# Score banks that accumulate on with differences of keys in four of eight rounds of a chunk

## What is computed

```python
h = _ln(x, g1, be1)
x = _attn(h, h, Wq1, Wk1, Wv1, Wo1, bo1) + x          # self-attention, 1024 keys
h = _ln(x, g2, be2)
x = _attn(h, context, Wq2, Wk2, Wv2, Wo2, bo2) + x    # cross-attention, 64 keys
h = _ln(x, g3, be3)
a, gate = split(h @ Wp + bp)
x = a * gelu(gate) @ W2 + b2 + x
```

## Time and profile before

| | |
|---|---|
| median of 3 runs | 2003.01 us (2002.07 to 2003.58) |
| the profiled execution's own time | 2002.8 us |
| its span, first to last instruction | 2001.0 us |
| PE / DVE / ACT / POOL busy, share of the span | 99% / 69% / 56% / 74% |
| granted TensorE clock | 1.000 |

### The profile page before, as it was taken

How to read it: one execution, slowest core, us unless ns; L and a number is a source line. 1 busy time by engine, 2 the same in 40 slices (tenths; PEclk the granted TensorE clock), 3 DMA queues, 4 the chain that set the end, 5 groups by cost and what they waited for, 6 DMA issues and landing times.

```text
span 2001.0 us, 32764 instructions
## 1 busy us (share of the span) xinstructions
PE 1990.7 (99%) x12568; PEld 1397.1 (70%) x12568; DVE 1382.0 (69%) x2766; ACT 1127.5 (56%) x1914; POOL 1489.8 (74%) x800
## 2 busy tenths in 40 slices
PE   9999999999999999999999999999999999999999
PEld 7665666666665666765666666665669999888888
DVE  6687687676767785587687666757767888744443
ACT  6565566554556665465566554556656776533332
POOL 3699899978989998899899889989897675300000
PEclk9999999999999999999999999999999999999999
DMA  8201000001000000010000001000030520000100
GB/s 275 85 32 38 6 7 17 8 25 48 17 12 6 17 6 27 1 64 6 7 18 10 27 1 53 7 27 1 22 104 10 158 69 1 1 22 28 37 12 32
DMA packets 48956, 67.19 MB, mean 34 GB/s; under 512 B 6176, under 2 KB 42144, under 8 KB 46752
## 3 DMA queue, kind: packets, MB, share of 16 engines
q1 hardware_dynamic: 48800, 65.10, 10.2%
HBM read 45.17 MB, written 19.92 MB: 33 GB/s over the span
## 4 chain that ended last, share of the span: by engine, by line
PE 94%; POOL 3%; DVE 2%; issue 1%; ACT 1%; DMA 0%; SPq 0%; POOLq 0%; DVEq 0%
PE score L559 21%; PE score L542 17%; PE score L685 9%; PE score L546 6%; PE score L497 5%; PE attn_project L699 5%; PE attn_project L670 5%; PE score L640 4%; PE attn_project L497 4%; PE first_score L523 4%; PE score L509 3%; PE attn_project L523 2%; POOL acc L1489 2%; PE score L608 2%; PE attn_project L608 2%; PE attn_project L509 2%
## 5 line engine op out<-in xcount | busy, mean ns | idle before, releaser
L1489 POOL TENSOR_TENSOR acc<-acc,pT 128x1024 f32<-128x1024 f32 x384 | 917.6, 2389 | 54.7 <-POOL acc L1489 1.3
L1233 ACT ACTIVATE pT<-score 128x1024 f32<-128x1024 f32 x512 | 525.3, 1027 | 141.1 <-PE score L546 100.3
L542 PE MATMUL score<-qk 64*128 64x512 f32 x3072 | 460.1, 399 | 0.4 <-ACT pT L1233 0.4
L559 PE MATMUL score<-pT,vT 128*64 128x512 f32 x1952 | 432.3, 595 | 0.0
L873 DVE TENSOR_REDUCE nmax<-first_score 128x1 f32<-128x512 f32 x512 | 347.8, 679 | 1.9 <-PE first_score L523 1.5
L873 DVE TENSOR_REDUCE nmax<-attn_project 128x1 f32<-128x512 f32 x512 | 347.7, 679 | 0.0
L542 PEld LDWEIGHTS score<-qk 64*128 64x128 f32 x3072 | 263.0, 185 | 107.5 <-ACT pT L1233 59.1
L559 PEld LDWEIGHTS score<-pT,vT 128*64 128x64 f32 x1952 | 134.6, 137 | 265.5 <-issue 245.4
L867 DVE SCALAR_TENSOR_TENSOR qk<-score,qk 128x512 fp32r<-128x512 f32 x66 | 45.6, 690 | 302.2 <-ACT qk L1214 302.2
L523 PE MATMUL attn_project<-qk 64*128 64x512 f32 x512 | 205.2, 401 | 3.4 <-DVE qk L867 3.4
L546 PE MATMUL score<-shift,pick 64*128 64x512 f32 x1024 | 208.4, 389 | 0.0
(11 more groups left out here) (196 smaller groups left out, 3135.8 us busy)
## 6 DMA issues: line engine op xcount, KB each, us to landing
xres<-x_middle SPq DMA_DIRECT2D x10, 512.0 KB, 3.7
raw_qk<-in_L_xattn_Wq SPq DMA_DIRECT2D x32, 128.0 KB, 2.3
raw_qk<-in_L_xattn_Wk SPq DMA_DIRECT2D x32, 128.0 KB, 2.5
raw_v<-in_L_xattn_Wv SPq DMA_DIRECT2D x8, 512.0 KB, 4.7
keys_all<-keys SPq DMA_DIRECT2D x1, 4096.0 KB, 13.1
values_all<-values SPq DMA_DIRECT2D x1, 4096.0 KB, 14.1
out_x<-xres SPq DMA_DIRECT2D x7, 512.0 KB, 2.9
xres<-in_x SPq DMA_DIRECT2D x3, 1024.0 KB, 6.6
```

The lines of the kernel that those rows point to most:

```text
L542: e.matmul(bank, qk[P % 2][r, 2 + h, keys], qk[P % 2][r, w, queries], start=(part == 0), stop=False)
L559: last = e.matmul(banks[bank][head * DH:(head + 1) * DH, :], vT[:, v_slot(D, jt), c0:c0 + DH], pT[:, jt, head, :], start=(jt == 0), stop=( ...
L1233: e.activation(pT[:, jt].rearrange("p h n -> p (h n)"), SC[R % 2][:, :], ACT.Exp).then_inc(s.exponential, 1)
L1489: e.tensor_tensor(total, total, pT[:, jt], ALU.add).then_inc(s.probs_added, 1)
```

## The change

A softmax numerator is `exp(score - max)`. In rounds 0, 1, 4 and 5 of a chunk the bank is started afresh and gets the shift, as before. In rounds 2, 3, 6 and 7 the same bank, which after the exponential still holds the shifted scores of the key tile two before, is not cleared: three pairs of matmuls with the **difference** of the key tiles (keys of jt minus keys of jt - 2) are accumulated on top, and the shift is not added again.

For this the split of a half of keys is made in more steps. ACT copies the first 256 columns in full to a new tile `keys_full`, and all 512 as leading parts (used by the rough scores and by the fresh tiles). DVE takes the rest of the first 256 columns, and subtracts `keys_full` from the last 256 columns in the PSUM bank. ACT rounds these differences, and DVE takes their rest. The queries' split stays as it was. The keys' projection moves from S1b to T1 and the sums' product from T1 to S1b, and to the head of the slot. Tiles are laid out anew, and three small ones are shared or cut (`ones`, `stats`, the order of `shift`).

```diff
@@ def slot(C):
+            if 1 <= C < NC - 1:
+                jobs += [("sum", C - 1, "S1b")]
             jobs += [(*job, through[i % len(through)]) for i, job in enumerate(between)]
             after = P + 1 + c
             if after < B * PAIRS:
-                jobs += [("qk", after, 1 - c, "S1b")]
-            if 1 <= C < NC - 1:
-                jobs += [("sum", C - 1, "T1")]
+                jobs += [("qk", after, 1 - c, "T1")]
             if after < B * PAIRS:
                 jobs += [("qk", after, 3 - c, "PJ")]
@@ first_score, tensor
-                need.wait_ge(s.split_hi, qk_of[P, half])
+                need.wait_ge(s.keys_rounded, keys_of[P, half])
@@ score, tensor
+                fresh = jt % TPC < 2
...
-                    e.matmul(bank, qk[P % 2][r, 2 + h, keys], qk[P % 2][r, w, queries], start=(part == 0), stop=False)
-                else:
+                    last = e.matmul(bank, key_part(P, h, r, jt), queries1[P % 2][r, w, c * BANK:(c + 1) * BANK],
+                                    start=(fresh and part == 0), stop=(not fresh and part == len(TERMS) - 1),
+                                    skip_group_check=not fresh)
+                elif fresh:
...
-                    e.matmul(bank, pick[r, :], shift[r, :], start=False, stop=True).then_inc(s.scored, 1)
+                    last = e.matmul(bank, pick[r, :], shift[r, :], start=False, stop=True)
+                if part == len(TERMS) - (0 if fresh else 1):
+                    last.then_inc(s.scored, 1)
@@ vector
+            def change_keys(P, u, bank):
+                n, later = keys_of[P, u], banks[bank][:, PAIR:]
+                need.wait_ge(s.keys_rounded, n)
+                need.wait_ge(s.keys_copied, n)
+                e.tensor_tensor(keys_lo[P % 2][:, u, 0:PAIR], banks[bank][:, 0:PAIR],
+                                keys_hi[P % 2][:, u, PAIR:2 * PAIR].bitcast(F32), ALU.subtract)
+                e.tensor_tensor(later, later, keys_full[:, :], ALU.subtract).then_inc(s.keys_changed, 1)
+                need.wait_ge(s.keys_changed, n)
+                need.wait_ge(s.split_hi, qk_of[P, u])
+                e.tensor_tensor(keys_lo[P % 2][:, u, PAIR:], later, keys_hi[P % 2][:, u, 0:PAIR].bitcast(F32),
+                                ALU.subtract).then_inc(s.split_lo, 1)
@@ split_qk, scalar, for keys
+                need.wait_ge(s.keys_changed, keys_of[P, u] - 1)
+                e.copy(keys_full[:, :], banks[bank][:, 0:PAIR]).then_inc(s.keys_copied, 1)
+                e.copy(keys_hi[P % 2][:, u, PAIR:], banks[bank]).then_inc(s.keys_rounded, 1)
+                need.wait_ge(s.keys_changed, keys_of[P, u])
+                e.copy(keys_hi[P % 2][:, u, 0:PAIR], banks[bank][:, PAIR:]).then_inc(s.split_hi, 1)
```

More of the change, by code:

```diff
@@ L118, in block_kernel @@
         maxima = sb("maxima", [PART, 2, SQUARE])
-        ones = sb("ones", [PART, DH])
+        keys_full = sb("keys_full", [PART, BANK // 2])
         QB = BANK // SQUARE
@@ L123, in block_kernel @@
         rsum = sb("rsum", [PART, QB])
-        (oT, pT, vT, acc, _, qk1, sums, qk0, shift, maxima_T, raw_qk, wqk, raw_v, wv, wo1) = overlay(
+        (oT, pT, vT, acc, shift, qk1, sums, qk0, maxima_T, raw_qk, wqk, raw_v, wv, wo1) = overlay(
             ("oT", [PRING, N], F32),
@@ L141, in block_kernel, with key_part @@
             ("wo1", [PAIRS, DIM], F32R))
-        qk = (qk0, qk1)
+        PAIR = BANK // 2
+        queries1 = [tile[:, 0:2 * N].rearrange("p (w n) -> p w n", w=2) for tile in (qk0, qk1)]
+        keys_lo = [tile[:, 2 * N:3 * N].rearrange("p (c n) -> p c n", c=CHUNKS) for tile in (qk0, qk1)]
+        keys_hi = [tile[:, 3 * N:].rearrange("p (c n) -> p c n", c=CHUNKS) for tile in (qk0, qk1)]
+        def key_part(P, w, r, jt):
+            c, t = divmod(jt, TPC)
+            start = t * PART if w else (t + 2) % TPC * PART
+            return (keys_lo if w else keys_hi)[P % 2][r, c, start:start + PART]
         _, *places = overlay(("oT_kept", [PRING, N], F32),
@@ L276, in block_kernel @@
         qk_of = numbered((P, u) for P in range(B * PAIRS) for u in (0, 2, 1, 3))
+        keys_of = numbered((P, u) for P in range(B * PAIRS) for u in range(CHUNKS))
         def rows_there(key):
@@ L411, in rouse @@
                 for _ in range(n):
-                    e.matmul(banks["S1b"][0:DH, 0:DH], ones[:, :], ones[:, :], start=True, stop=True)
+                    e.matmul(banks["S1b"][0:DH, 0:DH], sums[:, 0, 0:DH], sums[:, 0, 0:DH], start=True, stop=True)
             def context_turn():
@@ L522, in first_score @@
                 for m, (w, h) in enumerate(FIRST):
-                    last = e.matmul(banks[bank], qk[P % 2][r, w, q0:q0 + PART],
-                                    qk[P % 2][r, 2 + h, half * BANK:(half + 1) * BANK],
+                    last = e.matmul(banks[bank], queries1[P % 2][r, w, q0:q0 + PART], keys_hi[P % 2][r, half, PAIR:],
                                     start=(m == 0), stop=(m == len(FIRST) - 1))
@@ L732, in _ @@
                         sum_quads(C - 1, "T0")
-                    for part in range(len(TERMS) + 1):
+                    for part in range(len(TERMS) + (jt % TPC < 2)):
                         for head in range(2):
@@ L776, in ln_stats @@
             def ln_stats(src, mv_of, key):
-                n, slot = stat_of[key], key[1] % TILES
-                need.wait_ge(s.ln_agg, n - TILES if n > TILES else 0)
+                n, slot = stat_of[key], stat_of[key] % TPC
+                need.wait_ge(s.ln_agg, n - TPC if n > TPC else 0)
                 e.bn_stats(stats[:, slot, :], src).then_inc(s.ln_stats, 1)
@@ L860, in turn_wq2, with split_queries @@
                                   banks[WQ2_BANKS[2 * k + 1]].rearrange("p (j n) -> p j n", j=4)).then_inc(s.wq2T_in_v, 1)
-            def split_qk(P, u, bank="PJ"):
[L863 to L868, removed]
+            def change_keys(P, u, bank):
[9 more added lines that the diff above has]
+                                ALU.subtract).then_inc(s.split_lo, 1)
+            def split_queries(P, u, bank):
+                span = slice((u - 2) * BANK, (u - 1) * BANK)
+                need.wait_ge(s.split_hi, qk_of[P, u])
+                hi, lo = (queries1[P % 2][:, w, span] for w in range(2))
+                e.scalar_tensor_tensor(lo, banks[bank], SCALE, hi.bitcast(F32), ALU.mult, ALU.subtract
+                                       ).then_inc(s.split_lo, 1)
+            def split_qk(P, u, bank="PJ"):
+                (change_keys if u < 2 else split_queries)(P, u, bank)
             def row_max(C, t, half, head):
@@ L1553, in _ @@
             FFN_SPLITS = [i for i in range(TILES + 6, NT) if i % TILES in (6, 7, 0)]
-            e.memset(ones[:, :], 1.0).then_inc(s.const, 1)
+            e.memset(sums[:, 0, 0:DH], 1.0).then_inc(s.const, 1)
             e.memset(ident[:, :], 0.0).then_inc(s.const, 1)
```

21 lines of the change are left out of this document (10 added, 11 removed).

## The result

The changed kernel takes **2008.39 us** (median of 9 runs, 2006.73 to 2008.98) against 2003.32 us (2002.07 to 2003.88, 9 runs) for the kernel before: ratio 1.0024, 95% interval 1.0015 to 1.0033. It is slower by 5.1 us. The forecast was 2010.5, in a range of 2000 to 2020. The profiled executions lie 4.3 us apart (spans of 2001.0 and 2005.3 us).

What follows compares the result with a forecast made beforehand. DVE's row maxima were taken to bound the score stage, PE 0.18 us behind; 9.6 - 2.1 - 0.4 + 0.3 - 0.5 + 0.8 = +7.7 us on 2002.8, rounded to 2010.5 us, range 2000 to 2020.

Steps and rivals of the forecast that it cites:

- The law: Attend starts no sooner than D + 7.74 us; D: first row maximum's start after p, a chunk's first score matmul.
- Rival 3: Score rounds: PE's saving comes through, a round takes 1.11 instead of 1.17 us; -31 us, 1972 us; chance 0.02.
- Shift pairs: Score rounds: 256 pairs go, 59.7 us of PE, counting only up to 0.18 us a chunk beside DVE's row maxima.
- The chain of splits: Slot's ACT and DVE steps put the first row maximum at 2.01, before 1.63: +0.20 us in 48 ordinary chunks, +9.6.
- rival 2: A wash: low split prices put the first row maximum between 1.80 and 1.93; 2001 to 2007 us; chance 0.24.
- The chunks behind an output projection: Six chunks whose splits end early: attend at 9.20 against 9.55, -0.35 us each, -2.1 us in all.
- Behind a layer norm: Seven chunks: the sums leave DVE's chain, new split steps enter; first row maximum 2.95 against 2.89, +0.05 each, +0.3 us.
- The chunk near the end: One chunk with no projections before it, taken to gain like those behind an output projection: -0.4 us.
- The last chunk: Fewer pairs a round and no row maxima; ACT's exponential and the bank hand-over set it: about -0.5 us.
- The prologue: Before the first chunk, three halves of keys split the new way, two more ACT instructions each: +0.8 us.
- Rival 1: First row maximum stays at 1.63, so faster; POOL's cycle takes half the late-stretch gain: 1993 to 1998 us; chance 0.09.
- The DRAIN rule: DVE neighbours would not overlap, 0.08 us more per pair: first row maximum at 2.09, 4 us more over the run.

Runs made afterwards that it cites:

- experiment 1: The changed kernel with the shift pairs back in all eight rounds and every bank started afresh, new keys' split kept: 2008.96 us, 1.0030.
- experiment 6: The changed kernel with each row maximum taken over 256 of its 512 columns: 1975.73 us, 0.9865.
- experiment 2: The kernel before with only rounds 2, 3, 6 and 7 accumulating on without a shift, plain keys, slot and splits untouched: 1991.37 us, 0.9940.
- experiment 3: The kernel before with only the sums' product moved ahead of the keys, to the slot's head: 1997.12 us, 0.9969.
- experiment 4: The changed kernel with keys kept plain and split as before, by one copy and one subtraction: 1977.89 us, 0.9872.
- experiment 7: The changed kernel with row maxima over 256 columns and POOL's split of the projection weights moved to ACT and DVE: 1973.85 us, 0.9856.
- experiment 8: The changed kernel with only POOL's split of the projection weights moved to ACT and DVE: 2009.77 us, 1.0034.

## Why the prediction was right, and where it was off

*The law.* Attend = D + 7.74 held in every run with full maxima wherever DVE limited, in chunks 1 to 60 (the chunks at either end have other distances; for one of them see below). Experiments 1 and 6 show it from both sides: PE work put back changed nothing, DVE work taken away moved attend by 0.6. Rival 3, PE's saving in full, is out.

*Shift pairs.* "They count only up to the 0.18 us": experiment 2 measured 9.36 for 9.55.

*The chain of splits.* This is the mis-sized term. It was put at D = 2.01 and measured 1.91, so 48 x 0.10 = +4.8 in place of +9.6. Step by step the starts were foretold as -1.29, -1.02, -0.38, -0.05, 0.49, 0.76, 0.91, 1.40, and came as -1.30, -1.03, -0.40, -0.06, 0.39, 0.66, 0.87, 1.30. Most of the error is in one price: the subtraction back into PSUM was taken as 0.50, "nearer to 0.55", and takes 0.42, the lower bound. The row that drew me up had per-partition operands; the result's place cost nothing. The measured D lies in rival 2's band (1.80 to 1.93, for which I gave 2001 to 2007 us), and the time in the main forecast's: the other terms below made up the difference.

*The chunks behind an output projection.* D 1.46 and attend 9.20 were forecast and measured: -0.35 in each of six.

*Behind a layer norm.* +0.05 forecast, +0.01 measured in chunk 13 (0.1 us over all). Experiments 3 and 4 show what this small number hides: the sum's new place gives 1.1 and the new split takes it again.

*The chunk near the end.* -0.4 forecast for chunk 62; attend there stayed at 9.97 to 9.98, with D = 1.46 before and after. I had taken it for a chunk like those behind an output projection, with its attend bound by D + 7.74. But its products with the values go into PV, a bank of the rough scores, and not into S0. They wait for the last maximum of that bank, the fourteenth (1457.08 + 0.68 = 1457.76), which lies 8.5 us behind D in both kernels, so PE had nothing to win; it only waits longer, 0.70 us for 0.35:

```profile
1457.08 0.68 DVE L900 TENSOR_REDUCE nmax<-attn_project 128x1 f32<-128x512 f32 x1
```

```profile
1457.81 1.51 PE L571 MATMUL attn_project<-pT,vT 128*64 128x512 f32 x6 [0.70 <-DVE nmax L900]
```

*The last chunk.* -0.5 forecast; its attend came 0.4 us later (11.14 us after p, before 10.73), because PE waits 2.35 us there for the folded sums, before 1.54. Then the granted clock fell to 0.50, the 1.2 GHz level, for 3.4 us from 1475.63 on, which it did not do before, and from the start of attend to the cross-attention's first product 8.36 us passed in place of 7.02. The cross-attention and what follows were 1.6 us shorter, so the span ended with little of this. No run isolates these 1.6 us.

```profile
1474.10 0.41 PE L582 MATMUL first_score<-folded,quads 128*128 128x32 f32 x2 [2.35 <-DVE folded L924]
```

```profile
1476.00:1478.00 2.00, 2.00 (x6) 0.53 (x6) 0.92 (x2) 1.47 (x2) 2.00 (x2) 0.50 0.05 7
```

The last row is a stretch of 2 us; the column behind the five engines (PE, PEld, DVE, ACT, POOL) is the granted clock.

*The prologue.* +0.8 forecast; p of chunk 0 went from 58.86 to 60.26, +1.4.

*The sum.* From chunk 0 to chunk 62, p moved from 1443.75 - 58.86 = 1384.89 us to 1447.83 - 60.26 = 1387.57, +2.7; 4.8 - 2.1 is +2.7. With the prologue it is +4.1 at p of chunk 62, and the span grew by 4.3. That 7.7 was forecast and 4.3 to 5.1 came is in part luck: the chain was 4.8 too dear in the sum, and the prologue (0.6), chunk 62 (0.4) and the end (0.7) took 1.7 of that back.

*Rival 1's cap.* I held that POOL would take about half of a gain in its late stretch. Experiments 2, 4 and 7 contradict it: POOL's lag reached the exponentials but hardly PE (1.1 us in experiment 4, 1.9 in experiment 6). With the rival's own D, 1.62, experiment 2 took 1991.37, 12 us less than before, so the gain of about 11 came without a cap. And in the new slot D without the new split was 1.46 and the time 1977.89, far under the 1993 to 1998 that I gave.

*The DRAIN rule.* The DVE rows after again have 0.34 between starts for subtractions of 0.42. "VectorE: DVE Perf Modes" in the Trainium skill, section "The DRAIN you can't avoid", taken by its first sentences, would have such neighbours not overlap. By the rows they overlap by 0.08, and the 2.09 it would have given for D is further from 1.91 than 2.01 was. The same section goes on: "A next op that is not held starts earlier". The prediction left that out, and the rows agree with it.

## What to carry to other kernels

Before pricing what a change takes from an engine, find which engine the stage's next step waits for, and how close the runner-up is: of 59.7 us taken from PE only 12 were there to be had. Then price the preparation the change adds by its place in the chain between two engines, not by its length; the same work in another order was 16 to 24 us cheaper here. When a chain ping-pongs, put independent work (the queries) into the other engine's turn and move what nobody waits for out of it. Count every kind of chunk: the few behind a layer norm, left out of three expectations, held 5 to 8 us.

## What the runs showed of the hardware

- A DVE subtraction of 256 fp32 columns with both inputs in SBUF took 0.41 us with POOL idle and up to 2.53 beside POOL's additions (middle value 1.19), ending 0.28 us behind the POOL instruction that it met; the 512-column one in experiment 8 had a mean of 1.62:

```profile
L901 DVE TENSOR_TENSOR wqk<-raw_qk,wqk 128x512 fp32r<-128x512 f32 x30 | 48.5, 1617 | 0.0
```

  The same subtraction with one input in PSUM stayed at 0.41 to 0.43 beside the same POOL work. The Trainium skill, "SBUF — State Buffer", section "Who interferes with whom", describes a pair of ports that DVE and POOL take exclusively, and for DVE's instructions with two inputs only where both are in SBUF; the trace agrees.
- A subtraction from PSUM back into the same PSUM columns took what one into SBUF takes (the first and third row end in SBUF):

```profile
L879 DVE TENSOR_TENSOR qk<-first_score,qk 128x256 fp32r<-128x256 f32 x61 | 25.8, 423 | 142.1 <-ACT qk L1246 142.1
L881 DVE TENSOR_TENSOR first_score<-first_score,keys_full 128x256 f32<-128x256 f32 x61 | 25.7, 422 | 0.0
L884 DVE TENSOR_TENSOR qk<-first_score,qk 128x256 fp32r<-128x256 f32 x61 | 25.9, 425 | 31.4 <-ACT qk L1248 31.4
```
- In the trace of the kernel after the granted TensorE clock was 1.000 in all but one stretch ahead of the last microsecond: 0.50 for 3.4 us from 1475.63 on, 1.5 us after PE had stood 2.35 us for the folded sums. In the kernel before, where PE stood 1.54 us at the same place, it stayed at 1.000 there. The wait alone does not decide it: at the same place it stayed at 1.000 in experiment 3 with a wait of 2.60 us, and fell in experiment 4 with one of 2.81.
